# A two-layer network with an expert part: the first batch's loads in runs of 4 KB, the first group by feature blocks, and another order of VectorE's and ScalarE's prologue

## The reference

```python
h = gelu(x @ W1 + b1)                      # W1 512 x 2048, exact gelu
shared = h @ W2 + b2                       # W2 2048 x 384
expert = h @ We[index] + be[index]         # We 8 x 2048 x 128, chosen by the batch's index
out = x + concat([shared, expert], -1)     # float32 throughout
```

## Time and profile before

| | |
|---|---|
| median of 3 runs | 1249.43 us (1248.45 to 1249.52) |
| the profiled execution's own time | 1250.4 us |
| its span | 1248.5 us |
| TensorE busy | 1236.8 us (99%) |
| VectorE busy | 940.9 us (75%) |
| ScalarE busy | 742.6 us (59%) |
| transfers | 64.45 MB, mean 52 GB/s |
| granted TensorE clock, mean | 0.997 |

### The profile page before, as it was taken

The page is one execution under the profiler, slowest core; times in us unless marked ns, Lnnn a source line. Parts: engine busy times, 40 slices in busy tenths (PEclk is TensorE's granted clock), DMA queues, the critical chain, the costliest instruction groups (busy, mean ns, idle before and its releaser), DMA issues.

```text
span 1248.5 us, 23812 instructions
## 1 busy us (share of the span) xinstructions
PE 1236.8 (99%) x9376; PEld 919.3 (74%) x9376; DVE 940.9 (75%) x1201; ACT 742.6 (59%) x944; POOL 0.2 (0%) x4
## 2 busy tenths in 40 slices
PE   8999999999999999999999999999999999999998
PEld 4446667877777777778777778777777777787775
DVE  6887658777688787787777687776887867877765
ACT  3755556556566665666656665565666656666553
POOL 0000000000000000000000000000000000000000
PEclk9999999999999999999999999999999999999999
DMA  7212323003030020201102020030200203011000
GB/s 271 100 38 90 110 68 96 7 2 102 0 101 0 8 93 0 101 0 37 64 0 101 0 67 34 0 101 0 101 0 9 92 0 101 0 42 59 1 35 35
DMA packets 25650, 64.45 MB, mean 52 GB/s; under 512 B 5136, under 2 KB 5136, under 8 KB 22416
## 3 DMA queue, kind: packets, MB, share of 16 engines
q1 hardware_dynamic: 25616, 63.99, 15.0%
HBM read 47.20 MB, written 16.78 MB: 51 GB/s over the span
## 4 chain that ended last, share of the span: by engine, by line
PE 96%; DVE 2%; DMA 1%; ACT 1%; issue 0%; SPq 0%; ACTq 0%
PE banks L1113 15%; PE banks L1114 15%; PE banks L1115 15%; PE out_ps L1115 9%; PE out_ps L1114 9%; PE out_ps L1113 9%; PE q_ps L1113 8%; PE q_ps L1114 8%; PE q_ps L1115 8%; DMA h_ring<-w_dram 1%; PE banks L1127 1%; DVE x_lo L683 0%; DVE w_lo L683 0%; PE q_ps L1127 0%; PE out_ps L1127 0%
## 5 line engine op out<-in xcount | busy, mean ns | idle before, releaser
L1113 PE MATMUL banks<-x_hi,w_hi 128*128 128x256 f16 (+1 forms) x1704 | 467.3, 274 | 4.4 <-DVE x_lo L683 2.4
L1115 PE MATMUL banks<-x_hi,w_lo 128*128 128x256 f16 (+1 forms) x1704 | 467.4, 274 | 0.0
L1114 PE MATMUL banks<-x_lo,w_hi 128*128 128x256 f16 (+1 forms) x1704 | 467.4, 274 | 0.0
L683 DVE SCALAR_TENSOR_TENSOR h_ring<-u,scale,h_ring 128x2048 f16<-128x2048 f32 x120 | 281.2, 2343 | 7.5 <-ACT h_ring L449 5.3
L516 ACT ACTIVATE kept<-banks 128x512 f32<-128x512 f32 x180 | 106.3, 591 | 167.0 <-PE banks L1115 167.0
L1113 PEld LDWEIGHTS banks<-x_hi,w_hi 128*128 128x128 f16 x1704 | 166.8, 98 | 49.9 <-issue 5.1
L1114 PEld LDWEIGHTS banks<-x_lo,w_hi 128*128 128x128 f16 x1704 | 166.8, 98 | 43.1 <-issue 0.3
L1115 PEld LDWEIGHTS banks<-x_hi,w_lo 128*128 128x128 f16 x1704 | 166.8, 98 | 21.9
L457 ACT ACTIVATE h_ring<-u,scale 128x2048 f16<-128x2048 f32 x56 | 112.1, 2002 | 96.7 <-DVE u L859 96.7
L547 ACT ACTIVATE u<-u,b_sb,undo 128x512 f32<-128x512 f32 x120 | 91.2, 807 | 121.6 <-DVE u L904 121.6
L891 DVE TENSOR_TENSOR u<-banks,kept 128x512 f32<-128x512 f32 x60 | 41.5, 692 | 157.8 <-PE banks L1115 148.8
(11 more groups left out here) (142 smaller groups left out, 1670.4 us busy)
## 6 DMA issues: line engine op xcount, KB each, us to landing
x_raw<-x_dram SPq DMA_DIRECT2D x64, 256.0 KB, 3.7
e_raw<-we_dram SPq DMA_DIRECT2D x16, 1024.0 KB, 4.7
out_dram<-x_raw SPq DMA_DIRECT2D x64, 256.0 KB, 2.4
h_ring<-w_dram SPq DMA_DIRECT2D x5, 1024.0 KB, 8.1
t_sum<-w2p_dram SPq DMA_DIRECT2D x2, 1024.0 KB, 4.8
w_sums<-w_dram SPq DMA_DIRECT2D x2, 768.0 KB, 14.6
h_ring<-w_dram SPq DMA_DIRECT2D x2, 512.0 KB, 8.1
x_raw<-w_dram SPq DMA_DIRECT2D x1, 1024.0 KB, 11.1
```

The lines of the kernel that those rows point to most:

```text
L683: return nc.vector.scalar_tensor_tensor(to, of, s, hi, ALU.mult, ALU.subtract)
L1113: nc.tensor.matmul(ps, hi, v_hi, start=start, stop=False, skip_group_check=True)
L1114: nc.tensor.matmul(ps, hi, v_lo, start=False, stop=False, skip_group_check=True)
L1115: return nc.tensor.matmul(ps, lo, v_hi, start=False, stop=stop, skip_group_check=True)
```

## The change

It has six parts.

1. x of batch 0 is loaded in two transfers of 512 KB, each with rows of 4 KB (two feature blocks), in place of four with rows of 2 KB.
2. W1's group 0 comes from a copy in DRAM of its own, `w1f`, that lies by feature blocks: the first transfer holds all that k = 0 and 1 need, the second k = 2 and 3. Both have rows of 4 KB.
3. `first_group` waits for both halves at k = 0 and k = 2 alone. x's total stands ahead of the first product and not behind it, W1's total ahead of the products of k = 2 and not behind the first of them. WARM is 36 instead of 44.
4. Later totals on TensorE: x_total(0) and the total of W1's groups 2 and 3 stand behind block 0 of group 1 (before: behind block 1), W2's total ahead of group 3 (before: behind its block 0), and e_total(0) behind block 1 of group 3 (before: block 2).
5. VectorE and ScalarE: `w1_top(2)` moves ahead of the splits of W1's group 1, `w2_top(0)` and the scales of W1's group 0 move back; the sums `add_s(0)` move ahead of `w2_split(2)`; `w2_split(3)` and `e_split(0, 3)` move from ahead of batch 1 to behind its first copy or sum and the split of h's group 3. In batch 1 `e_top` moves behind `s_split(1)`.
6. SyncE's queue: `reload_w1(1)` moves ahead of `load_expert(1)`.

```diff
-WARM = 44
+WARM = 36
...
-            for k in range(KC):
-                sp.dma_start(x_raw[:, 0, k], x[0, :, k]).then_inc(first_x_loaded[k], 16)
-
-            blocks, raw = w1[0].rearrange("p (a n) -> p a n", a=4), w1_raw(0).rearrange("p (a n) -> p a n", a=4)
-            sp.dma_start(raw[:, 0::3], blocks[:, 0::3]).then_inc(w1_loaded[0], 16)
-            sp.dma_start(raw[:, 1:3], blocks[:, 1:3]).then_inc(w1_rest_loaded, 16)
+            for k in range(2):
+                sp.dma_start(x_raw[:, 0, KH * k:KH * (k + 1)], x[0, :, KH * k:KH * (k + 1)]
+                             ).then_inc(first_x_loaded[k], 16)
+
+            half = 2 * BLOCK
+            sp.dma_start(w1_raw(0)[:, :half], w1f[:, :half]).then_inc(w1_loaded[0], 16)
+            sp.dma_start(w1_raw(0)[:, half:], w1f[:, half:]).then_inc(w1_rest_loaded, 16)
...
             reload_w1(0)
+            reload_w1(1)
             load_expert(1, 1, D)
-            reload_w1(1)
...
# ScalarE and VectorE, batch(b): behind keep(b, 0, 0) or c11(b, 0) and h_split(b - 1, 3)
+                if isinstance(b, int) and b == 1:
+                    w2_split(3)
+                    e_split(0, 3)
...
# VectorE, batch(b): e_top
-                e_top(b)
+                if not sums:
+                    e_top(b)
...
                 if sums:
                     s_split(1)
+                    e_top(b)
...
# VectorE, prologue
+            w1_top(2)
             w1_split(1, 0, 2)
             w1_split(1, 2, 2)
-            w1_top(2)
             w1_top(3)
             first_h_top()
-            w2_top(0)
             w1_scales(2, 7)
             w1_scales(3, 9)
             first_h_scale()
-            w1_scales(0, 13)
+            w2_top(0)
             w1_split(2)
             h_split(0, 0, 0)
             w1_split(3)
+            w1_scales(0, 13)
...
# TensorE, first_group
+                    if k % KH == 0:
+                        pe.wait_ge(first_x_loaded[k // KH], 16)
+                        pe.wait_ge(w1_loaded[0] if k == 0 else w1_rest_loaded, 16)
                     if k == KH:
-                        pe.wait_ge(w1_rest_loaded, 16)
+                        w1_total(0, 2)
...
+            pe.wait_ge(first_x_max_done, KC)
+            total(first_x_tops, first_x_max[:, :]).then_inc(first_x_all_done, 1)
             first_batch()
```

More of the change, by code:

```diff
@@ L69, with build @@
 TOP_SUMS, TOP = 12, 14
-def build(nc, x, idx, w1, w2, w2p, we, b1, b2, be, out):
+def build(nc, x, idx, w1, w1f, w2, w2p, we, b1, b2, be, out):
     with ExitStack() as ctx:
@@ L141, in build @@
         x_loaded = [sem("x_loaded_even"), sem("x_loaded_odd")]
-        first_x_loaded = [sem(f"first_x_loaded{k}") for k in range(KC)]
+        first_x_loaded = [sem(f"first_x_loaded{k}") for k in range(2)]
         w1_loaded = [sem(f"w1_loaded{d}") for d in range(D)]
@@ L626, in _ @@
             first_gelu(1, 0)
-            first_gelu(1, 1)
             w1_split(2)
             h_split(0, 0, 0)
+            first_gelu(1, 1)
             first_gelu(1, 2)
+            w1_split(3)
             first_gelu(1, 3)
-            w1_split(3)
             h_split(0, 0, 1)
@@ L635, in _ @@
                 first_gelu(2, c)
+            w2_split(0)
             first_gelu(3, 0)
-            w2_split(0)
+            w2_split(1)
             first_gelu(3, 1)
+            e_split(0, 0)
+            e_split(0, 1)
             first_gelu(3, 2)
-            e_split(0, 0)
-            w2_split(1)
-            e_split(0, 1)
             first_gelu(3, 3)
@@ L645, in _ @@
             w2_split(2)
-            e_split(0, 2)
             residual(0, 0)
@@ L653, in _ @@
                 x_split(1, 1, i)
-            w2_split(3)
-            e_split(0, 3)
+            e_split(0, 2)
             batch(1, 1, sums=True)
@@ L685, in first_x_top @@
             def first_x_top(k):
-                dve.wait_ge(first_x_loaded[k], 16)
+                dve.wait_ge(first_x_loaded[k // KH], 16)
                 top(first_x_max[:, k:k + 1], x_raw[:, 0, k]).then_inc(first_x_max_done, 1)
@@ L1080, in _ @@
             w1_split(0, 0, 3)
+            add_s(0)
             w2_split(2)
-            e_split(0, 2)
-            h_split(0, 2, 0)
             x_scales(1, 1)
@@ L1086, in _ @@
             x_split(1, 1, P2)
-            add_s(0)
+            h_split(0, 2, 0)
             s_split(0)
@@ L1117, in first_group @@
             def first_group():
-                raw = w1_raw(0).rearrange("p (a k j c) -> p a k j c", a=4, k=KH, j=2)
+                raw = w1_raw(0).rearrange("p (k c m) -> p k c m", k=KC, c=C)
                 for k in range(KC):
-                    pe.wait_ge(first_x_loaded[k], 16)
-                    if k == 0:
-                        pe.wait_ge(w1_loaded[0], 16)
+                    if k % KH == 0:
+                        pe.wait_ge(first_x_loaded[k // KH], 16)
+                        pe.wait_ge(w1_loaded[0] if k == 0 else w1_rest_loaded, 16)
                     if k == KH:
-                        pe.wait_ge(w1_rest_loaded, 16)
+                        w1_total(0, 2)
                     for c in range(C):
-                        last = nc.tensor.matmul(first_bank(c), raw[:, A_OP[c // 2][k // KH], k % KH, c % 2],
-                                                x_raw[:, 0, k], start=k == 0, stop=k == KC - 1)
+                        last = nc.tensor.matmul(first_bank(c), raw[:, k, c], x_raw[:, 0, k],
+                                                start=k == 0, stop=k == KC - 1)
                         if k == KC - 1:
                             last.then_inc(first_l1_done, 1)
[L1131 to L1135, removed]
             def first_layer1(d, c):
@@ L1301, in first_batch @@
                     first_layer1(1, c)
-                    if c == 1:
+                    if c == 0:
                         x_total(0)
@@ L1307, in first_batch @@
                     first_layer1(2, c)
+                pe.wait_ge(w2_max_done, D)
+                total(w2_tops, w_max[:, D:2 * D]).then_inc(w2_all_done, 1)
                 for c in range(C):
                     first_layer1(3, c)
[L1310 to L1313, removed]
+                    if c == 1:
                         e_total(0)
@@ L1348 @@
     w1 = w1[:, :, (0, 0, 1, 1), (0, 1, 1, 0)]
+    w1f = np.asarray(L0_cond_W1).reshape(KC, P, 2, D, 2, P)[:, :, :, 0].transpose(1, 0, 2, 3, 4)
     def by_group(a):
@@ L1366 @@
         "w1": w1.reshape(D, P, 4 * BLOCK),
+        "w1f": w1f.reshape(P, 4 * BLOCK),
         "w2": by_group(L0_cond_W2).reshape(D, P, C * SHARED),
```

## The result

| | before | changed |
|---|---|---|
| median (6 runs each) | 1249.22 us (1248.45 to 1250.10) | 1239.71 us (1239.22 to 1240.36) |
| profiled execution, its span | 1250.4 us, 1248.5 us | 1239.52 us, 1237.8 us |

The account below looks back on a forecast made before the run. TensorE was busy 1236.8 of 1248.5 us, so only its idle time and clock could give. 4.0 us (prologue) plus 6.1 us (batch 1) took 10.1 from the 1249.4 us median: 1239.3 us, range 1238.2 to 1240.6.

Parts of the forecast that it names:

- Nothing waits behind 105 us, so all is decided before.: TensorE from 105 us to the end: no wait, order unchanged, so changes in the first 105 us carry through unaltered.
- The loads: x's total at 7.9, first product at 8.1.: Prologue: 4 KB rows at 422 GB/s bring x and W1 sooner; first product starts 2.3 us earlier.
- the fixed 4.0 us: Prologue loads: estimated time for issue and landing, added to every transfer's bytes over its rate.
- Gap of 1.2 us, no fall of the clock, group 1 at 22.1.: First product: gap under the harmless 1.57 us, so 14.0 us for first_group; 4.0 us gained. Clock-fall rival: 0.09, costing 1.7 us.
- W1's total and x_total(0) just in time.: VectorE's prologue: both totals' inputs ready 0.4 us before TensorE arrives, so no loss.
- ScalarE and not `x_lo` held P6, because of `add_s(0)`.: Batch 1's P6: ScalarE's copy was late after idling for add_s(0)'s sums; moving them removes 2.37 us and 1.7 of clock.
- Batch 1 gives 6.1 us.: Batch 1: three waits and one clock fall go, 2.37 + 1.7 + 1.57 + 0.47 us. Rival, first wait stays: 0.05.
- Slower only if e_top is over 9 us late.: Rival, chance 0.03: late e_top holds up TensorE; all 10.1 us lost only at 9.2 us later than worked out.
- The sum in medians.: Whole kernel: 4.0 at the prologue plus 6.1 at batch 1, 10.1 us off the median, giving 1239.3 us.
- 2 x 1.7 us: TensorE's clock: one fall behind the first product and one at batch 1, each counted as 1.7 us to regain.

Follow-up runs that it names:

- e4: The changed kernel with 20 matmuls on ones in place of 36: 1242.17 us.
- e7: The changed kernel with add_s(0) back directly ahead of s_split(0), and w2_split(3) and e_split(0, 3) back ahead of batch 1: 1243.44 us.
- e5: The changed kernel with add_s(0) back directly ahead of s_split(0) on VectorE: 1243.73 us.
- e6: The changed kernel with w2_split(3) and e_split(0, 3) back ahead of batch 1 on both engines: 1239.72 us.
- e2: The changed kernel with the loads, first_group, place of x's total and 44 matmuls on ones of before: 1243.24 us.
- e9: The changed kernel with batch 1's e_top back ahead of add_s(1) and c22: 1244.72 us.
- e8: The changed kernel with SyncE's old order, load_expert(1) ahead of reload_w1(1): 1248.22 us.
- e3: The changed kernel with x still in two transfers, but in rows of 2 KB: 1241.96 us.
- e10: The changed kernel with W1's first half loaded by ScalarE's queue, as its first instruction, in place of SyncE's third: 1243.43 us.
- e1: The kernel before with parts 1 to 3 alone (loads, first_group, x's total first, 36 matmuls on ones): 1246.46 us.

## Why the prediction was right

- *Nothing waits behind 105 us, so all is decided before.* Right: 10.7 us at 93.62 against 104.34, 10.7 in the spans.
- *The loads: x's total at 7.9, first product at 8.1.* 7.29 and 7.97. x's second half was there by 5.98 and not at 6.5; W1's halves, forecast for 7.7 and 9.0, were used at 7.97 and 9.21. That they fit so well is in part luck: the rate was not 422 GB/s from the start but some 240 until 4 us, and the fixed 4.0 us, taken from the old loads, had that slow start in it.
- *Gap of 1.2 us, no fall of the clock, group 1 at 22.1.* 0.44 and 0.50 us around the total, granted clock 1.00, 22.13. e4 shows what a longer gap can cost. That a gap of 1.57 us did no harm before is not in the earlier trace rows, which end at 100 us, ahead of it; the stretch behind it bears it out:

```profile
100.00:110.00 10.00, 8.43 (x60) 1.00 0.31 107
```

- *W1's total and x_total(0) just in time.* x_total(0) was, with 0.2 us to spare: VectorE's part ends at 24.51, and the total stands at 24.72 without a gap. W1's total was not: VectorE's second maximum ends at 15.01 (forecast 14.7), TensorE was free at 14.92 (two products of 0.43 us each from 14.06), and the total stands at 15.16. The wait of 0.2 us is in no list, because the list counts from the modelled end of the product before.
- *ScalarE and not `x_lo` held P6, because of `add_s(0)`.* Shown by e7, where the profile names the copy and P6 starts 0.14 us behind its end, as it did before (85.84 and 85.99). The step said that w2_split(3) was part of it, and for the wait it is: with `add_s(0)` late, P6 waits with these splits ahead of the copy (e7) and doesn't with them behind it (e5). In time this move brings nothing, neither alone (e6) nor with the other.
- *Batch 1 gives 6.1 us.* 6.0 by e2, and 6.5 in the profiled executions (10.72 less the 4.18 that batch 1 starts earlier). The part that was missing: the idle time in the list is counted from the modelled end of the last matmul (0.38 us behind its start for 512 columns), while the next could start after 0.22. So each of the three waits cost about 0.16 us more than its row says. In the same way a wait of 0.17 us ahead of group 2 had not been in the list; it is the difference between 4.01 us at group 1 and 4.18 at batch 1.
- *Slower only if e_top is over 9 us late.* It was in time, by 0.5 us (forecast 0.8); e5 and e9 show that its place and its load are the next to bind, at 2.1 and 3.5 us of wait.
- *The sum in medians.* 10.1 forecast, 9.5 measured, 10.7 in the two profiled executions. The interval of the measured gain, 8.2 to 10.7 us, holds both, so between medians there is nothing left to explain for certain. The term that stands on the weakest ground is the clock: 2 x 1.7 us were counted in full from one execution of before, while its runs at a granted clock of 0.999 and 1.000 are only 1.1 us shorter than those at 0.997. If that is its true weight in a median, the forecast came out right by luck in part, since the waits gave 0.5 us more than their rows said.

## What to carry to other kernels

When TensorE is busy for 99%, look for the few places where it isn't and for stretches below full clock, and work out for each who is late, from the engine that waits back to the instruction that it waited for; moving one small group of sums was worth as much as the new loads (taken away from the changed kernel, 4.0 us in e5 and 3.5 in e2). When an instruction that releases a transfer is moved back, go through the queue behind that transfer too: a one-line order in it carried 8.5 us (e8). And a gap of 2 to 3 us on TensorE costs its clock only in some executions, so read that price from several runs and not from one profile; look at the same time how far the runs at full clock lie apart.

## What the runs showed of the hardware that was not expected

- Whether the clock falls does not follow from the gap's length alone: not after 2.73 us (e3), but after 2.67 (e2), 2.58 (e4), 2.37, 2.09 (e5) and 2.05 (e7). In before it fell only a good microsecond after the first product had started (granted clock 1.00 from 10 to 11 us, 0.68 from 11 to 12), in e4 ahead of it (0.71 from 7 to 8). One fall made `first_group` 1.5 to 1.6 us longer (before, e2, e10) or 2.6 (e4).
- At the very beginning the column of the granted clock doesn't tell the pace: it reads 1.00 from the start, but e4's 20 matmuls of 256 columns on ones took 3.71 us, 0.19 each, and the 16 more of the changed kernel 1.96, 0.12 each.
- From 2 to 4 us the loads move only 150 to 280 GB/s, with rows of 2 KB (before, e3) and of 4 KB (the changed kernel, e1, e4, e9, e10) alike. From 4 to 5 us rows of 4 KB reach 400 to 420 (the changed kernel, e1, e4, e9), but only 254 in e10.
- A transfer on ScalarE's queue beside SyncE's made x's first half 2.9 us later (e10).
